# First attention's opening: masks ahead of the up matrix and of the second queries, the matrix quantised in pieces inside the first batches

## The reference

```
x = x + attention0(layernorm(x), ctx, ctx, mask)    # 16 heads of 16; masked keys get -10000; softmax; no projections
x = x + feed_forward0(layernorm(x), w_gate, w_up, w_down)   # each matrix first quantised (below), activations to 16 bits
x = x + attention1(layernorm(x), ctx, ctx, ...)     # 16 heads of 64, with projections, then layernorm
x = x + experts(layernorm(x), ...)                  # 8 experts, top 1 by a router
```

## Time and profile before

| | |
|---|---|
| median of 3 runs | 1369.53 us (1366.06 to 1372.7) |
| profiled execution | 1370.34 us |
| its span, first to last instruction | 1368.5 us |
| busy PE / DVE / ACT / POOL | 1300.9 / 1112.5 / 1043.1 / 400.2 us |
| mean granted TensorE clock | 0.988 |
| attention0, about | the first 235 us |

### The profile page before, as it was taken

The page is one execution under the profiler, slowest core; times in us unless marked ns, Lnnn a source line. Parts: engine busy times, 40 slices in busy tenths (PEclk is TensorE's granted clock), DMA queues, the critical chain, the costliest instruction groups (busy, mean ns, idle before and its releaser), DMA issues. The chain is left out here.

```text
span 1368.5 us, 34415 instructions
## 1 busy us (share of the span) xinstructions
PE 1300.9 (95%) x11246; PEld 1131.8 (83%) x11246; DVE 1112.5 (81%) x1983; ACT 1043.1 (76%) x2720; POOL 400.2 (29%) x677
## 2 busy tenths in 40 slices
PE   5999999999999999999899999999999689999998
PEld 2666666778888778899899999999998589999998
DVE  6899996879758789487687877878778778888887
ACT  4888887566579877663888888888887568888886
POOL 5555553000011111004122222222222134455553
PEclk9999999999999999999999999999999789999999
DMA  8411162475178998756123333243430267111110
GB/s 268 132 41 42 56 206 86 142 271 204 46 224 269 291 291 291 244 176 225 45 88 111 106 124 113 87 141 104 151 101 17 94 249 289 51 49 45 57 49 14
DMA packets 103253, 191.12 MB, mean 140 GB/s; under 512 B 12226, under 2 KB 67549, under 8 KB 98528
## 3 DMA queue, kind: packets, MB, share of 16 engines
q1 hardware_dynamic: 92480, 155.93, 33.9%
q0 software_dynamic: 10464, 33.57, 8.5%
q10 hardware_dynamic: 192, 0.13, 0.0%
HBM read 124.30 MB, written 68.03 MB: 141 GB/s over the span
## 5 line engine op out<-in xcount | busy, mean ns | idle before, releaser
L2374 ACT ACTIVATE c_w_raw<-c_ps_score,c_neg_max 128x128 f32<-128x128 f32 x512 | 181.9, 392 | 35.2 <-DVE c_neg_max L2171 27.5
L2740 PE MATMUL d_ps_hT<-d_zT,d_w_tile 128*128 128x128 f32 x1248 | 148.3, 278 | 1.3 <-DVE d_zT L2851 1.3
L2740 PEld LDWEIGHTS d_ps_hT<-d_zT,d_w_tile 128*128 128x128 f32 x1248 | 144.9, 194 | 2.2 <-DVE d_zT L2851 2.1
L2374 ACT ACTIVATION_READ_ACCUMULATOR c_w_raw<-c_ps_score,c_neg_max 128x1 f32 x512 | 118.6, 232 | 0.0
L2753 PE MATMUL d_ps_y<-d_w_parts,d_hT 128*128 128x256 f32 x912 | 118.5, 286 | 0.0
L2929 ACT ACTIVATE d_h<-d_ps_hT,d_b1T 128x128 f32<-128x128 f32 x312 | 88.6, 367 | 37.1 <-PE d_ps_hT L2740 37.1
L2753 PEld LDWEIGHTS d_ps_y<-d_w_parts,d_hT 128*128 128x128 f32 x912 | 111.6, 191 | 0.0
L2012 PE MATMUL c_ps_proj<-c_xnT,ahead_wq 128*128 128x256 f32 x768 | 107.2, 289 | 0.0
L2871 DVE TENSOR_TENSOR d_w_parts<-d_w,d_w_parts 128x1024 fp32r<-128x1024 f32 x76 | 92.8, 1221 | 10.0 <-ACT d_w_parts L2944 10.0
L2051 PE MATMUL c_ps_aux<-ahead_wo_high,c_attnT 128*128 128x256 f32 x512 | 99.6, 288 | 1.0 <-DVE logits L2195 1.0
L2012 PEld LDWEIGHTS c_ps_proj<-c_xnT,ahead_wq 128*128 128x128 f32 x768 | 95.2, 189 | 5.1 <-issue 5.0
(11 more groups left out here) (350 smaller groups left out, 3642.2 us busy)
## 6 DMA issues: line engine op xcount, KB each, us to landing
keys_scratch<-b_out SPq DMA_DIRECT2D x64, 256.0 KB, 4.7
values_scratch<-b_out SPq DMA_DIRECT2D x64, 256.0 KB, 4.0
ahead_kT<-keys_scratch SPq DMA_DIRECT2D x16, 1024.0 KB, 6.2
d_w<-w_in SPq DMA_DIRECT2D x16, 1024.0 KB, 6.8
split_scratch<-b_split SPq DMA_DIRECT2D x12, 1024.0 KB, 5.1
c_v_more<-values_scratch SPq DMA_DIRECT2D x24, 512.0 KB, 4.1
a_w<-w_in SPq DMA_DIRECT2D x16, 512.0 KB, 6.5
b_ctx_high<-split_scratch POOLq DMA_DIRECT2D x16, 512.0 KB, 5.1
```

The costliest lines, as they stand in the source:

```text
L2374: last = act.activation(prob[:, n, j, :], ps_score[:, n % 2, j, :], ACT.Exp, bias=neg_max[:, n, j:j + 1], accum_out=row_sum[:, n, j:j + 1])
L2740: last = pe.matmul(ps_hT[:, f, :], w1_tile[:, half, k, n * P:(n + 1) * P], zT[:, s, k, :], start=(k == 0), stop=(k == ND - 1))
```

## The change

1. SP loads masks 0 ahead of w_up; x is loaded in six parts, (0,2) (2,4) (4,8) and then eights; the keys of batches 2 and 3 go ahead of x 4 to 7, and the first values behind it.
2. POOL fills neg_eye behind the first queries, and casts masks 0 ahead of the second queries.
3. PE's steps 0 and 1 are written out anew: one query is turned, masks and scores of batch 0, query 1, masks and scores of batch 1, queries 2 and 3, then the first transposes of batch 0's probabilities.
4. DVE makes the scale of w_up and half of the first multiply before step 0; behind step 0 the statistics of batches 2 and 3 and the other half; behind step 1 the statistics of batches 4 to 7; behind step 2 the rounding; behind steps 3 and 4 the two halves of the second multiply. The rounded values lie in the space of upT.

```diff
--- before.py
+++ after.py
@@ -127,7 +127,7 @@
         ps_out = psum("ps_out", [P, BANK])
         out_heads = ps_out[:].rearrange("p (h w) -> p h w", w=VW)
 
-        x_loaded = [sem(f"x_loaded{c}") for c in range(5)]
+        x_loaded = [sem(f"x_loaded{c}") for c in range(6)]
         v_loaded = [sem(f"v_loaded{c}") for c in range(4)]
         mask_loaded = sem("mask_loaded")
         keys_loaded = [sem(f"keys_loaded{s}") for s in range(2)]
@@ -174,7 +174,7 @@
         w_up, upT = weights
         w_sb = sb("w", [P, COLS])
         w_blocks = w_sb[:].rearrange("p (n k) -> p n k", k=BLOCK)
-        w_rounded = probT[:].rearrange("p q h k -> p (q h k)").bitcast(I16)[:, 0:COLS].rearrange("p (n k) -> p n k", k=BLOCK)
+        w_rounded = upT[:].rearrange("p k n -> p (k n)").bitcast(I16)[:, 0:COLS].rearrange("p (n k) -> p n k", k=BLOCK)
         w_scale = sb("w_scale", [P, COLS // BLOCK])
         w_inv = sb("w_inv", [P, COLS // BLOCK])
         w_banks = ps_score[:].rearrange("p a (b h) k -> p (a b) (h k)", h=HB)
@@ -193,7 +193,7 @@
         w_done = sem("w_done")
         w_turned = sem("w_turned")
         ahead_done = sem("ahead_done")
-        X_PARTS = ((0, 2), (2, 8), (8, 16), (16, 24), (24, 32))
+        X_PARTS = ((0, 2), (2, 4), (4, 8), (8, 16), (16, 24), (24, 32))
 
         def load_first_keys(engine, pair, slot, heads):
             engine.wait_ge(keys_zero, slot + 1)
@@ -227,16 +227,17 @@
 
                 load_x(0)
                 sp.dma_start(ident[:], eye).then_inc(ident_loaded, 16)
+                load_mask(0)
                 sp.dma_start(w_sb[:].rearrange("p (o i) -> p o i", i=D), w_up.rearrange("(o p) i -> p o i", p=P)).then_inc(w_loaded, 16)
-                load_mask(0)
                 load_first_keys(sp, 0, 0, range(0, HALF, 2))
                 load_x(1)
+                load_first_keys(sp, 1, 1, range(HALF))
+                load_x(2)
                 load_v(0)
-                load_first_keys(sp, 1, 1, range(HALF))
-                for c in range(2, 5):
+                for c in range(3, 6):
                     load_x(c)
-                    if c < 4:
-                        load_mask(c - 1)
+                    if c < 5:
+                        load_mask(c - 2)
 
                 def store_x1(b):
                     sp.wait_ge(x1_ready, b + 1)
@@ -298,8 +299,6 @@
                 pool.memset(v_ones[:], 1.0).then_inc(consts, 1)
                 pool.memset(neg_eye[:], 0.0).then_inc(consts, 1)
                 pool.wait_ge(consts, 4)
-                pool.affine_select(out=neg_eye[:], in_=neg_eye[:], compare_op=ALU.not_equal, fill=NEG, base=0,
-                                   pattern=[[0, HB], [-1, P]], channel_multiplier=1).then_inc(consts, 1)
                 def deviations(first, n, turn):
                     pool.wait_ge(mv0_done, first + n)
                     part = bass.ds(first, n)
@@ -356,8 +355,10 @@
 
                 deviations(0, 2, 1)
                 queries(0, 0, 0)
+                pool.affine_select(out=neg_eye[:], in_=neg_eye[:], compare_op=ALU.not_equal, fill=NEG, base=0,
+                                   pattern=[[0, HB], [-1, P]], channel_multiplier=1).then_inc(consts, 1)
+                masks(0)
                 queries(1, 1, 1)
-                masks(0)
                 deviations(2, 2, 2)
                 queries(2, 0, 2)
                 pool.wait_ge(v_loaded[0], 16)
@@ -469,20 +470,27 @@
                 def turn_weights(g):
 
                     if g == 0:
-                        pe.wait_ge(w_done, 6)
+                        pe.wait_ge(w_done, 8)
                     for q in range(HB):
                         k, o = divmod(HB * g + q, FF // P)
                         c = (o * ND + k) * P
                         last = pe.transpose(w_banks[:, g, q * P:(q + 1) * P], w_sb[:, c:c + P], ident[:])
                     last.then_inc(w_turned, 1)
 
-                pe.wait_ge(consts, 5)
+
                 pe.wait_ge(ident_loaded, 16)
                 turn_qy(0, 0)
-                turn_qy(1, 1)
+                pe.wait_ge(consts, 5)
                 pe.wait_ge(mask_ready, 1)
                 turns = [0]
-                for b in range(2 * UN):
+                for b in range(2):
+                    masks(b)
+                    scores(b, b)
+                    turn_qy(b + 1, 1 - b)
+                turn_qy(3, 1)
+                transposes(0, 0, 0)
+                transposes(0, 0, 1)
+                for b in range(2, 2 * UN):
                     step(b, b % UN)
                 with pe.Fori(2, NB // UN - 1) as i:
                     turns[0] = i
@@ -610,34 +618,53 @@
                     dve.wait_ge(ahead_done, b - 3)
                     dve.bn_aggr(mv_next[:, u, :], stats_next[:]).then_inc(mv0_done, 1)
 
-                def quantise():
-                    def wide(t):
-                        return t[:].unsqueeze(2).to_broadcast([P, COLS // BLOCK, BLOCK])
-
+
+                HALF_BLOCKS = COLS // BLOCK // 2
+
+                def wide(t, blocks):
+                    return t[:, blocks].unsqueeze(2).to_broadcast([P, HALF_BLOCKS, BLOCK])
+
+                def weight_scales():
                     dve.wait_ge(w_loaded, 16)
                     dve.tensor_reduce(w_scale[:], w_blocks, AX_X, ALU.max, apply_absolute_value=True).then_inc(w_done, 1)
                     dve.wait_ge(w_done, 1)
                     dve.tensor_scalar(w_scale[:], w_scale[:], 1.0 / W_MAX, TINY, ALU.mult, ALU.max).then_inc(w_done, 1)
                     dve.wait_ge(w_done, 2)
                     dve.reciprocal(w_inv[:], w_scale[:]).then_inc(w_done, 1)
+
+                def scale_weights(half):
                     dve.wait_ge(w_done, 3)
-                    dve.tensor_tensor(w_blocks, w_blocks, wide(w_inv), ALU.mult).then_inc(w_done, 1)
-                    dve.wait_ge(w_done, 4)
+                    blocks = slice(half * HALF_BLOCKS, (half + 1) * HALF_BLOCKS)
+                    dve.tensor_tensor(w_blocks[:, blocks], w_blocks[:, blocks], wide(w_inv, blocks), ALU.mult).then_inc(w_done, 1)
+
+                def round_weights():
+                    dve.wait_ge(w_done, 5)
                     dve.tensor_scalar(w_rounded, w_blocks, W_MAX, -W_MAX - 1.0, ALU.min, ALU.max).then_inc(w_done, 1)
-                    dve.wait_ge(w_done, 5)
-                    dve.tensor_tensor(w_blocks, w_rounded, wide(w_scale), ALU.mult).then_inc(w_done, 1)
+
+                def unscale_weights(half):
+                    dve.wait_ge(w_done, 6)
+                    blocks = slice(half * HALF_BLOCKS, (half + 1) * HALF_BLOCKS)
+                    dve.tensor_tensor(w_blocks[:, blocks], w_rounded[:, blocks], wide(w_scale, blocks), ALU.mult).then_inc(w_done, 1)
 
                 dve.wait_ge(x_loaded[0], 16)
                 statistics(0, 2)
-                quantise()
-                dve.wait_ge(x_loaded[1], 16)
-                statistics(2, 4)
+                weight_scales()
+                scale_weights(0)
                 for b in range(2 * UN):
                     step(b, b % 2, b % UN)
                     if b == 0:
+                        dve.wait_ge(x_loaded[1], 16)
+                        statistics(2, 4)
+                        scale_weights(1)
+                    if b == 1:
+                        dve.wait_ge(x_loaded[2], 16)
                         statistics(4, 8)
+                    if b == 2:
+                        round_weights()
+                    if b in (3, 4):
+                        unscale_weights(b - 3)
                     if b == UN - 1:
-                        for c in range(2, 5):
+                        for c in range(3, 6):
                             dve.wait_ge(x_loaded[c], 16)
                 with dve.Fori(2, NB // UN - 1) as i:
                     for u in range(UN):
```

## The result

The changed kernel takes 1372.71 us in the median of 19 runs, the kernel before 1370.25 in 19 runs beside them. The ratio is 1.0026, with a 95% interval of 1.0018 to 1.0034: 3.6 us slower (2.5 to 4.7), less than the 0.5% that the prediction took as the limit of what can be told from no change; with 19 runs on each side the interval leaves out 1 nevertheless. The profiled execution took 1373.29 us with a span of 1371.5, so 3.0 more in span than the one before.

A forecast was written before the change was run, and what follows sets the result against it. It took the DVE, ACT and PE loop of the first attention as the bound, with late fourth masks delaying batch 4. 2.8 + 0.15 + 0.25 = +3.2 us on 1369.53 gave 1372.7, range 1367.0 to 1377.0.

The forecast's parts named there:

- The matrix lands when the masks did, 10.03: Opening loads: with masks ahead of it, the matrix lands at 10.03 us instead of 7.72.
- The half multiply alone, 0.88: DVE before batch 0: half the first multiply runs without POOL beside it, 0.88 us, giving first maxima at 13.45.
- PE's scores at 12.8: PE in the opening: batch 0's scores are ready at 12.8 us, before DVE's first maximum at 13.45.
- 7.44 from batch 0 to 1: First attention: the distance from batch 0's maxima to batch 1's stays 7.44 us, putting batch 1 at 20.9.
- Batch 2 at 26.8 to 27.7: First attention: batch 2's maxima come at 26.8 to 27.7 us instead of 29.44, with PE at 2.4 GHz.
- rival (c): Costlier opening: masks land with the matrix (+1.4 us), or PE stays longer at 1.2 GHz; about 1374.5 us, chance 0.15.
- Statistics at 24.95: DVE behind batch 1's subtraction: statistics of batches 4 to 7 start at 24.95 us, 5.1 later than before.
- Fourth masks issued at +10.35, landed at +15.15: SyncE's queue: times counted from the start of the statistics of batches 4 to 7; landing at 40.1 us.
- Waits of DVE beside POOL, 0.25 in all: DVE's moved multiplies: waits for POOL instructions, 0 to 1.04 us each, taken as 0.25 us in all.
- From batch 4 to 5, 0.15 more: DVE between batch 4's and 5's maxima: the other half multiply makes the distance 0.15 us longer.
- The gate at query 4: PE waits for query 4, ready at 30.5 us; arriving at 29, its gain of about 2 us falls to 0.9.
- The ruler: Starts of batches' first maxima on DVE: the whole time moves by their shift once the pattern repeats, some 50 us in.

The follow-up runs named there:

- e1: Changed kernel with the statistics of batches 4 to 7 back behind batch 0 on DVE; ratio to the kernel before 0.9990.
- e5: Changed kernel with POOL's cast of the fourth masks one step later, behind batch 0's inverse deviation; ratio to the kernel before 0.9995.
- e6: Changed kernel with the edits of e1, e2 and e5 together; ratio to the kernel before 0.9978.
- e3: Kernel before with only the statistics of batches 4 to 7 moved from behind batch 0 to behind batch 1; ratio to the kernel before 1.0025.
- e9: Kernel before with only POOL's casts of the second and fourth masks moved as in e6; ratio to the kernel before 1.0010.
- e2: Changed kernel with POOL's cast of the second masks ahead of the deviations of batches 4 to 7; ratio to the kernel before 0.9993.
- e4: Changed kernel with rounding and second multiply of the matrix moved behind batch 31; ratio to the kernel before 1.0017.
- e8: Changed kernel with the matrix loaded ahead of the first masks, as in the kernel before; ratio to the kernel before 1.0034.
- e7: Changed kernel with the edits of e6 and e4 together; ratio to the kernel before 0.9988.
- e10: The same kernel as e6, measured a second time; ratio to the kernel before 0.9987.

## Why the prediction was right

It forecast 1372.7, +3.2 us. The median was 1372.71, and +3.6 (2.5 to 4.7) by ratio. That the medians meet to 0.01 is luck: the forecast started from 1369.53, a median of 3 runs, and the kernel before has 1370.25 in 19. Point by point:

- *The matrix lands when the masks did, 10.03.* It landed at 10.84, and in the other runs with that order of loads at 9.29 to 11.46. Right in kind (same bytes ahead), off by 0.8 in this profile; my row was one draw.
- *The half multiply alone, 0.88.* It took 0.96. First maxima at 14.21 and not 13.45, 2.1 early and not 2.9.
- *PE's scores at 12.8.* Masks started at 9.11 as computed, but PE waited for the last keys (0.91) and ended at 13.98, still ahead of DVE. The prediction had no such wait; it had cover.
- *7.44 from batch 0 to 1.* 7.46. Batch 2 at 26.8 to 27.7: 27.33, at the high rate. In e1, whose first two places agree within 0.02, it came at 28.78: PE's transposes ahead took 1.91 instead of 1.04 and its masks 1.49 instead of 1.04. PE's half of rival (c) happens or not from profile to profile.
- *Statistics at 24.95.* 25.53, by the late matrix.
- *Fourth masks issued at +10.35, landed at +15.15.* Issued at +10.31, landed by +14.2. Batch 4's maxima were to start at 45.2 and did at 45.26, since this error of 0.9 and those of other signs cancel.
- *Waits of DVE beside POOL, 0.25 in all.* Undersized, and in another place: normalise took 0.81 beside POOL's addition instead of 0.40, the multiply behind batch 3 1.27 instead of 0.88 (in e5 and e6 it took 1.03, so 0.15 of this was there without any waiting), so from normalise to batch 4's maxima lie 2.38 and not 1.9. Rounding took 1.58 beside POOL's cast (0.95 in e6), off the path but for 0.2.
- *From batch 4 to 5, 0.15 more.* It was 1.45 more. This is the term that failed: I did not follow PE through the wait. DVE was through 6.41 us after batch 4's first maximum, as computed (6.5), but then waited 1.37 for PE, which had been idle for 2.84 and ran slowly behind it. The low clock stood among the rivals, at batch 2 and at another price.
- *The gate at query 4.* PE waited 1.75 for it and was at 31.20, 0.3 before its old place, not 0.9.
- *The ruler.* Batch 27 4.01 late, the whole 3.6 (2.5 to 4.7). Over the ten runs, the shift of batch 27 in the one profile and that of the total by ratio lie 0.5 to 3.0 us apart (e3 5.2 late and 3.4 slower, e6 0.0 and 3.0 faster, e9 0.5 early and 1.4 slower). So the ruler tells the late kernels from the others, but no difference of 1 or 2 us.

So the mechanism stands, by four runs from different sides: the statistics alone bring the loss (e3), putting them back removes it (e1), and so do two moves on POOL that leave the statistics late (e2, e5). The sum was right in part by cancelling: statistics 0.6 later than computed and 0.5 more behind normalise, against masks that landed 0.9 sooner; then PE's wait of 1.37, against the 0.25 for POOL and the 0.3 that the ruler gave back behind batch 5. On the ruler it was 4.0 and not 3.2.

That PE slows because of its pause was not tried alone. In batch 5 the two go together in every profile: with 2.84, 1.77, 1.94 and 2.75 us of pause ahead of batch 5's masks (after, e3, e4, e8) masks and scores of that batch are slow (masks 1.83 to 1.89, in e3 the scores, 2.09); in before, e1, e2, e5, e6, e7, e9 and e10, with 0.38 at most, masks take 1.04 in each. Elsewhere they don't: behind a pause of 1.78 in before (batch 2), of 1.89 in e9 (batch 2) and of 1.75 in the kernel after (31.20 above) masks took 1.04, 1.04 and 1.03, and behind one of 2.31 in e3 (batch 2) 1.89. So behind a pause of about 1.8 us either rate was seen, and what decides stays open.

## What to carry to other kernels

Follow a moved instruction through every in-order queue that waits for it, the DMA issuer's too: statistics that PE wants only as query 4, two batches on, held a cast, the cast held a load, the load held another cast, and behind that stood a small operation that everyone needed. Before moving work later, look for the wait that stands ahead of urgent work without being urgent itself: putting the cast of masks for batches 24 to 31 behind the deviation of batch 0 cost nothing and gave back 4 us. A stall can cost more than its length: in the kernel after, PE ran slowly behind its pause of 2.84 us, and DVE waited another 1.37 for it.

## What the runs showed that I had not expected

- The time at which the same load lands differs by more than 2 us between single profiles of kernels whose first loads are the same: the matrix at 9.29 (e4), 9.42 (e10), 10.21 (e2), 10.76 (e7), 10.84 (after, e5), 10.86 (e1) and 11.46 (e6). One profile can't price an opening closer than that.
- PE's rate in batch 2 is not set by the instructions alone: e6, e7 and e10 issue the same up to there, and batch 2's masks took 1.58, 1.04 and 1.90. From batch 1's maxima to batch 2's lie 7.17, 5.67 and 7.23 us, so this moves batches 2 and later by up to 1.6 from one profile to the next. From 24 to 28 us the granted clock is 0.57 in e10 and 1.00 in e7, but 1.00 in e6 too, where the transposes took 1.92 and the masks 1.58: durations showed the slow stretch there, the granted clock did not, and that it was the lower clock is not shown.
- Where DVE multiplies or rounds from SBUF to SBUF beside POOL, the later of the two seems to wait for the earlier: in e5 the copy of values takes 1.13 instead of 0.40, begun at 42.11 inside DVE's multiply (41.95 to 42.98). The Trainium skill (SBUF — State Buffer, section "SBUF: two separate sides") describes such turns at a shared port; by that rule, the trace agrees with these rows. The rows also show the size: the later one lost what it overlapped with the earlier, less 0.13 to 0.15 us, in the first multiply (0.85 of overlap and 0.70 lost in before, 0.38 and 0.23 in e3, 0.51 and 0.36 in e9, against the second multiply's 1.76, and 0.43 and 0.28 in e8, against 0.96), in the rounding (0.77 and 0.63 after, 1.00 and 0.87 in e5, against 0.95) and in that copy (0.87 and 0.73). Normalise beside POOL's addition lost less, 0.41 of 0.66.
